# One cross-attention layer on one core: when a context piece is rounded, where two query heads stand, and when the first output products run

## The reference, cut to what matters

```
q = (layernorm(x) @ Wq + bq).reshape(B, L, NKV=8, G=4, HDIM=128)
k, v = split(ctx @ Wkv + bkv)                      # 6272 keys, 8 kv heads
scores = einsum('blkgd,bmkd->bkglm', q, k) * scale
o = einsum('bkglm,bmkd->blkgd', softmax(scores), v)
x = x + o @ Wo + bo
```

## Time and profile before

| | us |
|---|---|
| runs | 1017.62, 1019.71 and 3386.0, median 1019.71 |
| profiled execution | 1017.49 |
| its span | 1015.7 |
| TensorE busy | 996.8 (98% of the span) |
| VectorE, ScalarE, GpSimd busy | 744.5, 587.4, 441.6 |

### The profile page before, as it was taken

The page is one execution under the profiler, slowest core; times in us unless marked ns, Lnnn a source line. Parts: engine busy times, 40 slices in busy tenths (PEclk is TensorE's granted clock), DMA queues, the critical chain, the costliest instruction groups (busy, mean ns, idle before and its releaser), DMA issues.

```text
span 1015.7 us, 20355 instructions
## 1 busy us (share of the span) xinstructions
PE 996.8 (98%) x7083; PEld 922.3 (91%) x7083; DVE 744.5 (73%) x1680; ACT 587.4 (58%) x1254; POOL 441.6 (43%) x641
## 2 busy tenths in 40 slices
PE   8989999999999999999999999999999999999998
PEld 6769999999999999999999999999999999999744
DVE  5677877676877777777877778677777768776666
ACT  5455666565656656566665656565665655565431
POOL 2243544444434545344454445434444444333231
PEclk9999999999999999999999999999999999999999
DMA  9763332333424333333333333333333237464895
GB/s 323 229 218 128 107 129 98 133 120 131 138 93 134 106 129 112 113 131 130 129 107 115 107 133 122 125 118 117 128 107 133 93 125 245 161 220 157 254 329 162
DMA packets 90085, 149.59 MB, mean 147 GB/s; under 512 B 10528, under 2 KB 44976, under 8 KB 89984
## 3 DMA queue, kind: packets, MB, share of 16 engines
q1 hardware_dynamic: 88224, 146.42, 43.6%
q10 hardware_dynamic: 1424, 1.51, 0.4%
q0 software_dynamic: 336, 0.35, 0.1%
HBM read 82.97 MB, written 14.81 MB: 96 GB/s over the span
## 4 chain that ended last, share of the span: by engine, by line
PE 91%; DVE 4%; DMA 2%; ACT 1%; issue 1%; SPq 1%; POOL 0%; DVEq 0%; POOLq 0%; ACTq 0%
PE p_kv L88 16%; PE p_kv L90 16%; PE p_kv L89 15%; PE p_s L88 7%; PE p_s L90 6%; PE p_s L89 6%; PE p_t L769 6%; PE p_o L88 4%; PE p_o L90 4%; PE p_o L89 4%; PE p_s L849 1%; PE p_ot L753 1%; DMA wkv_raw<-in_wkv 1%; DMA ctx_st<-in_ctx_t 1%; PE p_o L783 1%
## 5 line engine op out<-in xcount | busy, mean ns | idle before, releaser
L610 POOL TENSOR_SCALAR slots<-code 128x512 f32<-128x512 bf16 x232 | 147.8, 637 | 247.3 <-DVE slots L1466 164.2
L1210 ACT ACTIVATE pt_hi<-p_t 128x512 fp32r<-128x512 f32 x224 | 110.0, 543 | 117.0 <-PE p_t L769 111.4
L1466 DVE TENSOR_TENSOR slots<-slots 128x512 f32<-128x512 f32 x232 | 169.8, 732 | 1.6 <-POOL slots L610 1.5
L1239 ACT ACTIVATE slots<-code,drop_and_offsets 128x512 f32<-128x512 bf16 x232 | 158.6, 713 | 6.5 <-POOL code L606 3.4
L1198 ACT ACTIVATE v_hi<-p_kv 128x256 fp32r<-128x256 f32 x196 | 75.3, 384 | 139.1 <-PE p_kv L90 138.3
L630 POOL TENSOR_TENSOR slots<-slots 128x512 f32<-128x512 f32 x58 | 77.7, 1339 | 165.5 <-DVE slots L1466 165.5
L1430 DVE TENSOR_TENSOR pt_lo<-p_t,pt_hi 128x512 fp32r<-128x512 f32 x224 | 128.7, 614 | 11.0 <-ACT pt_hi L1210 10.0
L1415 DVE TENSOR_TENSOR v_lo<-p_kv,v_hi 128x256 fp32r<-128x256 f32 x196 | 83.1, 424 | 67.4 <-ACT v_hi L1198 64.7
L88 PE MATMUL p_kv<-wkv_hi,ctx_even_hi 128*128 128x256 f32 x448 | 128.9, 288 | 0.2 <-DVE v_lo L1415 0.2
L89 PE MATMUL p_kv<-wkv_lo,ctx_even_hi 128*128 128x256 f32 x448 | 125.9, 281 | 0.0
L90 PE MATMUL p_kv<-wkv_hi,ctx_even_lo 128*128 128x256 f32 x448 | 125.9, 281 | 0.0
(11 more groups left out here) (261 smaller groups left out, 2717.5 us busy)
## 6 DMA issues: line engine op xcount, KB each, us to landing
probs_r<-probs SPq DMA_DIRECT2D x110, 448.0 KB, 3.7
code<-in_codes SPq DMA_DIRECT2D x58, 256.0 KB, 3.8
scale<-in_scales SPq DMA_DIRECT2D x114, 128.0 KB, 3.1
expanded_weights<-slots SPq DMA_DIRECT2D x56, 256.0 KB, 2.1
ctx_st<-in_ctx_t SPq DMA_DIRECT2D x96, 112.0 KB, 3.0
ring_hi<-expanded_weights SPq DMA_DIRECT2D x22, 256.0 KB, 5.4
ring_lo<-expanded_weights SPq DMA_DIRECT2D x22, 256.0 KB, 5.6
wq_hi<-in_wq SPq DMA_DIRECT2D x4, 1024.0 KB, 7.2
```

The costliest lines, as they stand in the source:

```text
L610: nc.gpsimd.tensor_scalar(slots[:, slot, :], code16[:], LINES[j][0], LINES[j][1], ALU.mult, ALU.add).then_inc(pool_lines, 1)
L1210: nc.scalar.activation(pt_hi[:, at:at + n, :].rearrange("p t q -> p (t q)"), p_t[:, c % 2, 0:n * ROWS], ACT.Copy).then_inc(pt_rounded, 1)
L1239: nc.scalar.activation(slots[:, slot, :], code16[:], ACT.Identity, bias=offsets[:, k:k + 1], scale=LINES[j][0]).then_inc(act_lines, 1)
L1466: nc.vector.tensor_tensor(slots[:, slot, :], slots[:, slot, :], slots[:, other, :], ALU.max).then_inc(merged, 1)
```

## The change

Three edits, none of which adds or removes an instruction except one load slot that becomes empty:

```diff
-    elif pair < 2:
-        piece = ((0, 1, PIECES, 2, 3), (4, PIECES, 5, 6, 7))[pair][place]
+    elif pair == 0:
+        piece = (0, 1, PIECES, PIECES, 2)[place]
...
                 next_keys(i, h, half, 0)
+                weigh_values(i - 1, 0, SPLIT_TILE)
                 if i == 2:
                     query_product(7)
-                weigh_values(i - 1, 0, SPLIT_TILE)
...
                 for t in value_tiles(i)[:SPLIT_TILE]:
+                    if i == 2 and t == 2:
+                        query_turn(7)
                     value_tile(i, h, half, t)
-                if i == 2:
-                    query_turn(7)
...
                 turn_attention(1)
-                project_out(0)
                 weigh_values(i - 1, 0, SPLIT_TILE)
                 turn_probs(i - 1, 2)
                 turn_probs(i - 1, 3)
+                project_out(0)
                 project_out(1)
...
                 split_probs(i - 1, 1)
+                if i == 2:
+                    finish_query(6)
                 merge(i, 0)
...
                 merge(i, 2)
-                if i == 2:
-                    finish_query(6)
...
+                if i == 2:
+                    finish_query(7)
                 for t in tiles[3:]:
                     split_values(i, t)
                 split_keys(i, h, 1)
                 if i == 2:
-                    finish_query(7)
                     add_output(0, 0)
```

## The result

The changed kernel took 1011.92 us (median of 5 runs, 1010.28 to 1012.59). The kernel before, run beside it, took 1021.52 (median of 5, 1017.62 to 1021.84 without one run of 3386). The ratio is 0.9924, with a 95% interval of 0.9902 to 0.9945: faster by 0.5 to 1.0%, which is inside 2%. The ratio leaves the run of 3386 out and is not the quotient of the two medians. The forecast was 1011.2. The span of the profiled execution fell from 1015.7 to 1010.1, by 5.6 us where the sum had said 6.3.

What follows compares the result with a forecast made beforehand. TensorE, busy 98% of the span, was taken as the bound. Gains of 5.0, 0.9 and 0.4 us summed to 6.3, taken from the profiled 1017.49 to give 1011.2 us, with a range from 1008.8 to 1016.

Steps and rivals of the forecast that it cites:

- the sum: Whole kernel: 5.0 us up to block 2's queries, 0.9 at turn_output(0), 0.4 in the last block, 6.3 in all.
- The first wait: End of block 1: TensorE's 2.26 us stall for k_lo goes, with 1.3 us to spare.
- late next: Block 1: transposes and score statistics, needing the copied probabilities landing at 64.6, run from 64.6 to 65.3.
- The new place of piece 2: End of block 1: piece 2, queued behind the codes, lands at 65.4, giving a new 1.4 us stall before weigh_values(1).
- the rival of the early landing: End of block 1: piece 2 lands by 64.0, no new stall, 7.7 us won, 1009.8 us; chance 0.2.
- the 5.0: Blocks 1 and 2: query_product(7) with weigh_values(1) begins at 69.2 instead of 74.20, 5.0 us won.
- 3.5 us to the moved piece: Block 1: with piece 2 moved, the next keys start at 65.3 in place of 68.84, 3.5 us won.
- 2.9 to the queries: Block 2: the old 2.54 us stall before query_product(7) goes, 2.9 us with its edges.
- less 1.4: Block 2: a new 1.4 us stall before weigh_values(1), from piece 2 landing at 65.4, taken off the gain.
- that rival: Block 2: query_product(7)'s wait merely moves, finish_query(6) still needing late VectorE; counted as 1.4 us, no chance given.
- a clock term: Block 1: the low clock behind the stall for k_lo costs 1.4 us, and goes with that stall.
- The last block: Start of the last block: TensorE starts 0.4 us earlier, at 943.97; at least nothing, at most 1.32 won.

Runs made afterwards that it cites:

- the piece alone: Kernel before with only the context pieces' new table, queries and last block as before: 1018.32 us, ratio 0.9992.
- the queries alone: Kernel before with only query_product(7), query_turn(7), finish_query(6) and finish_query(7) moved as in the change: 1013.62 us, ratio 0.9949.
- without the pieces: Changed kernel with the old table of context pieces put back: 1013.25 us, ratio to before 0.9949.
- bias of query 6 alone: Kernel before with only finish_query(6) moved ahead of VectorE's maxima in block 2: 1015.00 us, ratio 0.9955.
- query 7's turn alone: Kernel before with only query_turn(7) and finish_query(7) moved earlier, the turn ahead of the third value tile: 1018.10 us, ratio 0.9989.
- product of query 7 alone: Kernel before with only query_product(7) moved behind weigh_values(1): 1016.30 us, ratio 0.9979.
- last block alone: Kernel before with only the last block's order changed, project_out(0) put behind weigh_values and two turn_probs: 1020.03 us, ratio 0.9996.

## Why the prediction was right, point by point

**The sum.** 1011.2 forecast, 1011.92 and 1011.55 measured. In the profiles, 5.6 us of 6.3: block 3 starts 4.96 earlier (5.9 forecast) and the last block gives 0.4 (0.4). The 0.9 missing at block 3 has one place. `weigh_values(1)` starts at 70.17, not 69.2, because piece 2 landed at 66.4 instead of 65.4. The probabilities, at 65.4 instead of 64.6, would by themselves have made it 69.7, by the 0.44 that VectorE waited for ScalarE. Everything behind it runs as forecast.

**The first wait.** `k_hi` and `k_lo` ended at 61.15 and 61.86 (61.1 and 61.8 forecast). The stall went, the clock stayed at 1.00, and "late next" was right: the transposes wait for the copied probabilities.

**The new place of piece 2.** The queue ahead of it set its landing, as argued. By the rule of the Trainium skill's page "DMA: Bandwidth & Descriptors", section "Queues, rings and completion order", the piece isn't counted before the codes; it came 0.4 behind them here, and its landing moved with the queue. One sentence was wrong: the stall before `weigh_values(1)` does not grow "one for one" from a landing at 64.0. VectorE's statistics wait for the probabilities, and by the rows above they hold some 0.8 of the 1.26 by themselves. So the rival of the early landing had not 1.4 us to win but some 0.4, unless the probabilities came earlier too.

**The split of the 5.0.** This is where the working was weakest. It booked 3.5 us to the moved piece and 2.9 to the queries, less 1.4. By the runs the piece alone is worth nothing that can be measured (0.9992), the queries alone 0.5%. The first wait covers the second in the same queue: take away only the first (2.26), and the second grows by as much (4.89 for 2.54), with the slow clock behind it. The prediction named that rival ("the wait of `query_product(7)` merely moves") for the change as a whole and had it in its sum as the 1.4; it happens in full when the piece is moved alone. On top of the queries the piece gives 1.7 us by the medians, which the intervals do not separate from nothing.

**The clock.** 1.4 us of the 3.5 was slow clock behind the stall for `k_lo`. That was a property of one execution: the same wait, 2.82 long without the pieces and 2.74 with the bias of query 6 alone, left the clock at 1.00. In the blocks as before it fell at the first wait in one profile (2.26) and at the second in another (4.62), so the sum held a clock term of the right size for a reason that the next execution need not show.

**The median.** The forecast stood on a profile 2.2 us under the median and took the difference for noise. The runs of before lie between 1016.5 and 1021.8 in all comparisons, those of the change between 1010.3 and 1012.7. Two profiles of the same code (39.4 and 42.0 us in blocks 1 and 2) show a part of that spread in these two waits, and the clock at the start of the program another. Against the median the change is worth 7 to 8 us by its ratios, more than 6.3; how much of the surplus is longer waits in other executions of before was not measured. That 1011.2 came within 0.7 us of the result is in part luck: a base below the median and a sum below the gain against the median made up for each other. The remark that 2% is about what a measurement can tell from no change was wrong: the intervals here are 0.2 to 0.4% wide.

**The last block.** 0.4 in the profiles; by the times of the runs it can't be seen.

## What to carry to other kernels

When an in-order engine has several waits on the same path, price them as one: remove the first alone and the next takes over its length, so start with a later one (here the bias of query 6, 4.6 us alone), or remove them together. In these runs a small load landed right behind the load issued before it (0.3 to 0.4 us behind the codes with the queue as in the change), and took 3.1 and 4.0 us instead of 7.8 and 6.6 with the 1 MB of `load_wq(7)` and the codes issued behind it; if an engine's whole queue stands at such a load, issue it ahead of the megabytes that nobody waits for yet. And before a stall's slow clock is booked as a gain, look at a second execution.

## What the runs showed of the hardware

How long TensorE idles did not by itself decide its clock. In blocks 1 and 2 it fell from 2.4 to 1.2 GHz after idle stretches of 2.12 (query 7's turn alone), 2.26 (before), 2.38 (product of query 7 alone), 4.62 and 4.89 us; it stayed at 2.4 GHz after 2.54 (before), 2.65 (query 7's turn alone), 2.74 (bias of query 6 alone) and 2.82. In one and the same execution (before, and query 7's turn alone) it fell after the shorter stretch and not after the longer one. Where it fell ahead of `query_product(7)`, its sixteen products took 3.32 to 3.68 us instead of 1.95. At the start of the program TensorE idles 1.37 us, up to 18.2 to 19.1 us, in all fourteen profiled executions. In seven of them the clock was 0.50 from 20 to 22 us, in the others it stayed at 1.00; the work from there to the next wait took 6.6 us (last block alone) instead of 5.1 (before).

A load of 112 KB took from 2.0 us to land (before) to 11.1 (bias of query 6 alone). With the 1 MB of `load_wq(7)` and the codes ahead of it, piece 2 took 7.8 and 6.6 us, and 3.1 and 4.0 with both behind it. SP's own issue of such a load took 0.33 us at 67.65 and 1.35 at 58.60 in the changed kernel; what sets this, no run here shows.
